# The attention's softmax sums as fp32 products in quarters of the array, from exponentials kept whole

## The reference, cut to what matters

```
x = x + attention(layernorm(x), context)      # 32 query heads, 8 key heads, head size 128
x = x + ffn(layernorm(x))                     # x @ W_base.T + b, plus the low-rank part of 2 of 8 experts
attention: logits = 30 * tanh(q.k * 0.0884 / 30), masked
           weights = exp(logits) / sum(exp(logits))       # over the 128 context positions of a batch
           out = (weights @ v) @ Wo
```

## Time and profile before

| | |
|---|---|
| median of 3 runs | 2163.47 us (2162.84 to 2166.55) |
| profiled execution | 2166.17 us, of which its span 2164.4 us |
| granted TensorE clock, mean of the span | 0.998 |
| PE busy | 2147.4 us, 9437 matmuls |
| DVE / ACT / POOL busy | 1669.5 / 880.1 / 259.8 us |
| softmax sums (L915, L917) | 128 + 128 matmuls, 50.6 + 50.4 us busy |

### The profile page before, as it was taken

The page is one execution under the profiler, slowest core; times in us unless marked ns, Lnnn a source line. Parts: engine busy times, 40 slices in busy tenths (PEclk is TensorE's granted clock), DMA queues, the critical chain, the costliest instruction groups (busy, mean ns, idle before and its releaser), DMA issues.

```text
span 2164.4 us, 26519 instructions
## 1 busy us (share of the span) xinstructions
PE 2147.4 (99%) x9437; PEld 1768.8 (82%) x9437; DVE 1669.5 (77%) x2570; ACT 880.1 (41%) x1342; POOL 259.8 (12%) x296
## 2 busy tenths in 40 slices
PE   9999999999999999999999999999999999999999
PEld 7888888888888888877888888888888888888887
DVE  6976888888886666667777788988988888857443
ACT  3313243222241111146555556655665566424221
POOL 0350001111130000011101111101111111100000
PEclk9999999999999999999999999999999999999999
DMA  9798697666596666699666875688667854696751
GB/s 331 240 344 265 223 335 271 221 232 221 196 339 225 209 209 219 217 276 262 180 184 193 253 233 158 210 273 258 187 192 251 278 180 153 210 371 255 292 186 66
DMA packets 208883, 508.50 MB, mean 235 GB/s; under 512 B 20592, under 2 KB 54000, under 8 KB 206704
## 3 DMA queue, kind: packets, MB, share of 16 engines
q1 hardware_dynamic: 196464, 472.67, 64.6%
q0 software_dynamic: 12288, 34.14, 5.6%
HBM read 357.26 MB, written 149.16 MB: 234 GB/s over the span
## 4 chain that ended last, share of the span: by engine, by line
PE 95%; DMA 3%; DVE 1%; ACT 1%; issue 0%; SPq 0%; POOL 0%; ACTq 0%; DVEq 0%
PE ps L379 30%; PE ps L380 30%; PE ps L381 30%; PE ps L915 1%; PE ps L917 1%; DMA qD<-qt 1%; DMA rD<-r 0%; DMA kraw<-ctxT 0%; PE ps L1182 0%; PE ps L1181 0%; DMA raw<-gran 0%; DMA qf<-qD 0%; DVE Rl L329 0%; ACT Rh L325 0%; DMA raw<-ctxT 0%
## 5 line engine op out<-in xcount | busy, mean ns | idle before, releaser
L379 PE MATMUL ps<-Ah,Rh 128*128 128x512 f32 x1024 | 400.6, 391 | 0.0
L380 PE MATMUL ps<-Al,Rh 128*128 128x512 f32 x1024 | 399.5, 390 | 0.0
L381 PE MATMUL ps<-Ah,Rl 128*128 128x512 f32 x1024 | 398.8, 389 | 0.0
L380 PE MATMUL ps<-Xq,qW 128*128 128x512 f32 x896 | 348.5, 389 | 0.0
L381 PE MATMUL ps<-Xq,qW 128*128 128x512 f32 x896 | 348.5, 389 | 0.0
L379 PE MATMUL ps<-Xq,qW 128*128 128x512 f32 x896 | 348.5, 389 | 0.0
L325 ACT ACTIVATE Rh<-raw 128x1024 fp32r<-128x1024 f32 x176 | 186.3, 1059 | 169.6 <-PE ps L381 148.4
L329 DVE TENSOR_TENSOR Rl<-raw,Rh 128x1024 fp32r<-128x1024 f32 x172 | 209.2, 1216 | 41.1 <-ACT Rh L325 40.8
L981 DVE TENSOR_TENSOR Y<-ps,Y 128x512 f32<-128x512 f32 x256 | 175.8, 687 | 82.2 <-PE ps L381 81.0
L381 PEld LDWEIGHTS ps<-Ah,Rl 128*128 128x128 f32 x1024 | 192.2, 188 | 42.3
L379 PEld LDWEIGHTS ps<-Ah,Rh 128*128 128x128 f32 x1024 | 192.1, 188 | 41.9
(11 more groups left out here) (218 smaller groups left out, 3912.7 us busy)
## 6 DMA issues: line engine op xcount, KB each, us to landing
raw<-gran SPq DMA_DIRECT2D x177, 512.0 KB, 4.4
QSD<-qW SPq DMA_DIRECT2D x64, 512.0 KB, 3.6
qD<-qt SPq DMA_DIRECT2D x128, 256.0 KB, 3.2
qW<-QSD SPq DMA_DIRECT2D x64, 512.0 KB, 3.6
qf<-qD SPq DMA_DIRECT2D x64, 512.0 KB, 6.7
RB<-rD POOLq DMA_DIRECT2D x128, 256.0 KB, 8.5
qraw<-gran SPq DMA_DIRECT2D x48, 512.0 KB, 4.3
kD<-kst SPq DMA_DIRECT2D x32, 512.0 KB, 3.9
```

The lines of the kernel that those rows point to most:

```text
L379: put("pe", waits, lambda e: e.matmul(pe_out, lh, rh, start=first, stop=False, skip_group_check=more))
L380: put("pe", [], lambda e: e.matmul(pe_out, lh, rl, start=False, stop=False, skip_group_check=more))
L381: return put("pe", [], lambda e: e.matmul(pe_out, ll, rh, start=False, stop=last, skip_group_check=more), mark)
```

## The change

Three things are changed, and what follows from them:

1. The exponential (ACT) no longer goes back into PSUM but into a whole fp32 tile Pf in SBUF, which has the place of Pl. The high part Ph is copied from Pf. The score's PSUM bank is free when the exponential is done; before, when Ph and Pl were.
2. `att_den` is done once for a group: four products, one for each batch, with 32 columns of ones as weights on the fp32 tile Pf, each in another quarter of the array (`tile_position=(0, 32 * x)`) and so in other 32 rows of Tb. They wait for the exponentials alone. Pl is computed in Pf's place, by DVE or POOL, after these four, and the value products wait for it.
3. The step of the sums is now one number for each group: in the steady state it comes two steps behind the group's last score (before: each batch's sums three steps behind its score). The numbers of the first three groups are new.
4. The four small warm-up products are taken out.

```diff
@@ -348,9 +349,6 @@
-        for x in range(4):
-            put("pe", [m_sel, m_one], lambda e, x=x: e.matmul(ps[7][32 * x:32 * x + 32, 0:224], f(ones[:, 0:32]), f(sel[:, :]),
-                                                              start=True, stop=True, tile_position=(0, 32 * x)), None, 190)
@@ -900,23 +898,26 @@
-            a = put("act", [a], lambda e: e.activation(s, s, ACT.Exp, scale=CAP), ca)
-            h = put("act", [a] + p_free[z], lambda e: e.activation(Ph[z][:, :], s, ACT.Copy), ca)
-            l = put("dve", [h], lambda e: e.tensor_tensor(Pl[z][:, :], s, f(Ph[z][:, :]), ALU.subtract), cd)
-            sb_free[n] = [h, l]
-            p_marks[gi, b] = [h, l]
+            a = put("act", [a] + p_free[z], lambda e: e.activation(Pf[z][:, :], s, ACT.Exp, scale=CAP), ca)
+            sb_free[n] = [a]
+            h = put("act", [a] + p_free[z], lambda e: e.activation(Ph[z][:, :], Pf[z][:, :], ACT.Copy), ca)
+            e_marks[gi, b], p_marks[gi, b] = a, h
         def att_den(gi, b):
-            i, z = gi % 2, (4 * gi + b) % NP
-            w = sel[:, 96 - 32 * b:224 - 32 * b]
-            put("pe", p_marks[gi, b] + [m_sel] + (tb_free[0] if b == 0 else []), lambda e: e.matmul(
-                Tb[:, :], w, Ph[z][:, :], start=b == 0, stop=False))
-            md = put("pe", [], lambda e: e.matmul(Tb[:, :], w, Pl[z][:, :], start=False, stop=b == 3), cn("pe_den"))
-            if b < 3:
-                return
+            i = gi % 2
+            for x in range(4):
+                z = (4 * gi + x) % NP
+                md = put("pe", [e_marks[gi, x], m_one] + tb_free[0], lambda e, z=z, x=x: e.matmul(
+                    Tb[32 * x:32 * x + 32, :], f(ones[:, 0:32]), Pf[z][:, :], start=True, stop=True,
+                    tile_position=(0, 32 * x)), cn("pe_den"), 240)
+            for x in range(4):
+                z = (4 * gi + x) % NP
+                h = p_marks[gi, x]
+                p_marks[gi, x] = [h, lo(Pl[z][:, :], Pf[z][:, :], Ph[z][:, :], [h, md], "pl")]
@@ -936,7 +937,7 @@
-                      v_marks[gi] + ob_free[n], cn("pe_pv"))
+                      v_marks[gi] + p_marks[gi, b] + ob_free[n], cn("pe_pv"))
@@ -1100,16 +1101,16 @@
-        first = {0: ((-15, -14, -13, -12), (-11, -10, -10, -9), -8, (-5, -4, -3, -2)),
-                 1: ((-11, -9, -7, -5), (-8, -6, -4, -2), -2, (2, 3, 5, 6)),
+        first = {0: ((-15, -14, -13, -12), -11, -9, (-7, -6, -5, -4)),
+                 1: ((-11, -9, -7, -6), -4, -2, (2, 3, 5, 6)),
...
-            scores, sums, rows, values = first.get(gi, (range(z, z + 8, 2), range(z + 3, z + 11, 2), z + 11, range(z + 13, z + 21, 2)))
+            scores, sums, rows, values = first.get(gi, (range(z, z + 8, 2), z + 8, z + 11, range(z + 13, z + 21, 2)))
```

7 lines of the change are left out of this document (4 added, 3 removed).

## The result

The changed kernel takes 2158.16 us (median of 10 runs, 2155.18 to 2165.25), the kernel before 2164.02 beside it: a ratio of 0.997, with a 95% interval of 0.9958 to 0.9982. It is faster by 0.3%: 6 us where 27 were forecast, and 7 us above the range. The profiled execution took 2160.04 us with a span of 2158.2.

What follows compares the result with a forecast made beforehand. PE was taken as the bound, its time being instructions times their distance plus a few stalls. Terms -26 - 4 + 1 = -29 us from the profiled 2166.17 gave 2137, or 2134.5 from the median; forecast 2136, range 2126 to 2151.

Steps and rivals of the forecast that it cites:

- What bounds the kernel: Whole kernel: PE, busy 99% of the span, is the bound; its waits come to some 15 us.
- Term 1: Sums, 32 groups: four quarter products take 1.2 us instead of 2.02, saving 26 us (18 to 33).
- (a): Sums: quarters reading four different tiles are served one after another; about 2217 us, slower; chance 0.08.
- (b): Sums: quarters served two at a time or at half rate, no gain there; 2162 us; chance 0.05.
- Term 2: Attention's start: some 7.5 us of stalls removed, 3.5 to 4 added; -4 us, between -8 and 0.
- The old waits: Attention's start: PE's waits for rT (3.8 us) and late Pl (1.4) go, and most of an earlier Pl stall.
- the one for Rl: Attention's start, near 963 us: PE waits for the filler's last weights, 2 to 2.5 us of new stall.
- the chain through RB: Attention's start: chain from copy to first multiplication takes 18 us, started at some 954 ends at 972 to 973.
- about 1.5 us: Attention's start: new stall at the third value product, reached at 973 to 974, needing the first one's bank.
- Term 3: Second layer norm stretches: sums wait for the last exponential where DVE is nearly full; +1 us (0 to 4).
- Rival (c): All 32 groups: bursts of four Pl on DVE give back 0.5 us each, 16 us; 2152 us; chance 0.07.
- Costs named and put at nothing: ACT operations, Pl subtractions, ACT's SBUF reads, and the warm-up's 0.90 us, hidden behind the first input's wait: no cost.

Runs made afterwards that it cites:

- e6: Changed kernel with each packet's four quarter products issued twice: 2178.45 us.
- e4: Changed kernel, planner told that the filler's stores vD<-stg land 4.5 us later: 2154.44 us.
- e14: Changed kernel, order untouched, filler's stores read from xT so its copies into stg need not wait for them: 2148.42 us.
- e12: Changed kernel, order untouched; x1D<-Y stores and layer norm loads read xT, reloads of Y wait for the additions alone: 2152.5 us.
- e8: Changed kernel, planner told filler's stores land 4.5 us later and every DMA from the attention's fourth group on 2.9 us later: 2143.58 us.
- e1: Changed kernel with the old step numbers for the attention's first three groups: 2156.27 us.
- e9: Changed kernel, order untouched, only the second layer norm's loads read xT in place of x1D, not waiting for the stores: 2159.62 us.
- e15: Changed kernel, order untouched, filler's stores a quarter of their size and from xT: 2151.59 us.
- e18: Changed kernel itself measured once more, without edits (source of the second profile): 2156.7 us.
- e2: Changed kernel, planner told every DMA lands 5000 ns after issue instead of 2100: 2153.44 us.
- e10: e8 with the third and fourth of the attention's first four Y loads put 2 and 4 steps later: 2143.93 us.
- e11: e10 plus planner told that the last stores qD<-qt before the attention land 4.5 us later: 2144.42 us.
- e17: Changed kernel, order untouched, with the edits of both e12 and e14: 2149.06 us.
- e3: Changed kernel, planner told later landings (5.0, 4.0, 3.5 us) for three of the second layer norm's transfers alone: 2164.82 us.
- e5: Changed kernel with the sums again eight fp32r products on Ph and Pl, in one row at the new step: 2162.93 us.

## Why the prediction was wrong

- **What bounds the kernel: right, and not enough.** PE's waits were read and sized; SyncE's own waits (25.1 us for the store x1D<-Y, above) and the DMA share of the start (0.97 and 0.89) were not read. The earlier trace rows show a DMA share of 0.74, and the text used only DVE's busy time from them. The list of PE's waits comes to 13.6 us, not to 15; nothing hangs on that.
- **Term 1: right.** 1.2 us forecast for a packet, 1.23 measured; inside it 0.88 streaming (0.85 forecast), 0.09 way in (0.1), 0.22 way out and slow next product (0.24), the rest on neighbours. 25 us saved where 26 were forecast. Halves of a packet are 0.45 us apart. The Trainium skill, "TensorEngine Tiling (Array Packing)", Key Properties, has TensorE drained at a change of tiling mode: the row shows 0.09 us, not the 0.16 that it was given. Rivals (a) and (b) are out by e6.
- **Term 2: wrong in sign, -4 forecast, +4.4 measured (+3.3 in the second profile).** The old waits went as said, the one for Rl came with 2.9 us (2 to 2.5 forecast), the chain through RB ended at 972.8 (972 to 973). The step that failed is "about 1.5 us" for the third value product: it asked when RB lands and not what stands on ACT ahead of Ah. That was the filler's copy into stg, 6.9 us behind its store. The forecast moved a chain two steps ahead and did not look at what it now meets in each queue. e4 removes the 6.1 us by another order, e14 half of them by taking the wait away; neither wins all of it back, as the loads behind are late too.
- **Term 3: right as far as it went, but the larger cost was elsewhere; +1 forecast, +14.7 measured (+10.6).** The waits for Pf that it named came, larger than its 0 to 4: 5.4 us (5.9 in the second profile); e12 leaves 2.8 of them.

  The step that failed is that SyncE's queue was put at nothing, without a reason: no row of it was read, and DVE alone was asked what it could hold up. What cost most was SyncE standing at the reload Y<-xT until the store x1D<-Y had landed, with DVE's additions L<-Y in front of Al and Y: from 1020 to 1900 us, 20.6 us of DVE's waits, 38.3 of SyncE's, against 5.6 and 25.1 before. e12 takes it to 3 us, e8 to 0.9.

  The other profiles fit. The seven in which SyncE waits 36 to 40 us for the store (after, e1, e4, e9, e14, e15, e18) have 8.9 to 14.7 us beyond; the six with short groups in which it waits 11.4 us or less (e2, e8, e10, e11, e12, e17) have 0.6 to 3.4; e3 (27.6 us) has 18.9, by the waits for Pf told above. The two with longer groups have 1.6 (e5, 28.7 us) and 0.7 (e6, 15.5).

  The reload stood one issue behind its store in the kernel before too (store at 1689.43, reload at 1693.73, 4.3 us later; now 6.7): the weak place was there, at a cost that PE did not see. Why the stores land later now (x1D<-Y 9.0 us against 6.7, medians) is open; the issues' new spacing is a candidate, not shown.
- **Rival (c)** put a price of 16 us on the layer norm's neighbourhood, and the measured miss has nearly that size, but for bursts of Pl on DVE, in all groups. Plain groups lose nothing, and e12's groups have the same bursts.
- **Costs named and put at nothing: right.** The first product that needs the next input starts at 11.77 us, 11.76 before.
- **The range** ended at 2151 because each term was bounded by rows of PE, DVE and ACT in the old order. No term stood for what a planner makes of a change: three numbers in e3 changed DVE's order in over a hundred places, and kernels with the same work here lie between 2143.6 and 2164.8 us. That spread, some 20 us, is the size of the miss. The +4.4 and the +14.7 are the loss in one execution of one such order.

## What to carry to other kernels

A saving on the bounding engine was paid out here only where no other queue stood in the way: read the DMA share and the DMA issuer's own waits by stage, not only the compute engines'. Where a reload stands right behind the store that frees its buffer in one in-order queue, everything behind it pays the store's landing (6.2 us here); put other issues between them. When a scheduler re-derives the order, first judge the arithmetic (here 0.79 us a group, to a few hundredths), then the order for itself: a planner that takes 2.1 us and 3 ns a KB for a DMA, where its transfers of 256 and 512 KB take 5 to 13 us at the start and in the layer norm (medians), makes orders that are good by luck, and changing that one number moved one kernel by -5 us and the other by +37.

## What the runs showed of the hardware that was not expected

Four fp32 quarter products of 512 columns take 0.88 us side by side, as a second packet right behind a first shows, and 1.23 us with both ends between full products.

A DMA engine share above 1.0 with 309 to 315 GB/s went with no loss at all for PE (e12), and a share of 0.94 at 277 GB/s with stalls in the same two groups: the share alone does not say that a stretch is bound by DMA. The order of issue was the same in both; what differed is that SyncE stood still in one.

Issues to landing in the 80 us of the attention's start, before and after (out<-in, queue, count, KB each, median us), for two kinds of transfer:

```profile
raw<-gran SPq DMA_DIRECT2D x11, 512.0 KB, 8.2
...
Y<-xT SPq DMA_DIRECT2D x4, 512.0 KB, 9.2
```
```profile
raw<-gran SPq DMA_DIRECT2D x9, 512.0 KB, 11.6
...
Y<-xT SPq DMA_DIRECT2D x4, 512.0 KB, 13.0
```

They land 3 to 4 us later after the change, and so do qf<-qD and vD<-stg (10.4 us against 7.2, 9.4 against 5.8), but kT<-kD does not (8.0 against 8.9), at no more traffic (20.6 MB against 22.2 in that stretch). That they were issued closer together is a likely reason, not shown; how much is the change's and how much the execution's, one profile of each can't say.
